# The gate z and the folded weights moved between set-up and steps of a selective state block, on one core

## What is computed

```python
def _mamba2(x, Win, Wconv, bconv, dt_bias, A_log, D, gn_w, Wout):
    zxbcdt = x @ Win
    z = zxbcdt[..., :DIN]
    xBC = silu(_causal_conv(zxbcdt[..., DIN:DIN + CONVDIM], Wconv, bconv))
    xh, Bm, Cm = ...                      # parts of xBC
    dt = softplus(zxbcdt[..., -NHEADS:] + dt_bias)
    A = -exp(A_log)
    y = _ssd(xh, dt, A, Bm, Cm) + rev(_ssd(rev(xh), rev(dt), A, rev(Bm), rev(Cm)))
    y = y + D[None, None, :, None] * xh
    y = _rmsnorm(y.reshape(b, l, DIN) * silu(z), gn_w)
    return y @ Wout
def _ssd(xh, dt, A, Bm, Cm):
    cum = cumsum(dt * A, axis=1)
    decay = where(tril, exp(cum[:, :, None] - cum[:, None, :]), 0)
    return einsum('blsh,bshp->blhp', (Cm . Bm)[..., None] * decay * dt, xh)
```

## Time and profile before

| | |
|---|---|
| median of 3 runs | 2950.7 us (2944.52 to 2956.05) |
| profiled execution, its own time | 2953.49 us |
| its span | 2951.5 us |
| PE busy | 2153.9 us (73%), weight loads 1100.1 (37%) |
| DVE busy | 1981.8 us (67%) |
| ACT busy | 1744.2 us (59%) |
| POOL busy | 1079.7 us (37%) |
| mean granted TensorE clock | 0.857 |

### The profile page before, as it was taken

The page is one execution under the profiler, slowest core; times in us unless marked ns, Lnnn a source line. Parts: engine busy times, 40 slices in busy tenths (PEclk is TensorE's granted clock), DMA queues, the critical chain, the costliest instruction groups (busy, mean ns, idle before and its releaser), DMA issues. The chain is left out here.

```text
span 2951.5 us, 64266 instructions
## 1 busy us (share of the span) xinstructions
PE 2153.9 (73%) x26182; PEld 1100.1 (37%) x26182; DVE 1981.8 (67%) x2779; ACT 1744.2 (59%) x2811; POOL 1079.7 (37%) x827
## 2 busy tenths in 40 slices
PE   4277777776774887698688588658857886885886
PEld 3022222222221553354255245325524542552553
DVE  2587888888877566565666656565765666666564
ACT  1266766766653575477367457536754773674574
POOL 0044444444451343244045235304522531451342
PEclk6588888888896998799799799869978988997998
DMA  4000000000001111110111111011111101111111
GB/s 133 0 0 1 0 1 0 1 0 0 1 0 29 32 34 28 35 33 15 44 38 26 38 27 40 15 31 32 34 36 26 42 15 39 33 25 30 32 34 31
DMA packets 96695, 74.59 MB, mean 25 GB/s; under 512 B 69392, under 2 KB 77584, under 8 KB 95120
## 3 DMA queue, kind: packets, MB, share of 16 engines
q1 hardware_dynamic: 96400, 70.48, 10.0%
HBM read 20.62 MB, written 8.39 MB: 10 GB/s over the span
## 5 line engine op out<-in xcount | busy, mean ns | idle before, releaser
L892 POOL TENSOR_TENSOR SQ<-SQ 128x512 f32<-128x512 f32 x344 | 467.2, 1360 | 708.4 <-ACT SQ L811 425.1
L859 POOL TENSOR_TENSOR Y<-Z 128x512 f32<-128x512 f32 x256 | 330.8, 1292 | 531.6 <-DVE Z L1096 297.7
L807 ACT ACTIVATE O<-bank 128x512 f32<-128x512 f32 x512 | 304.3, 594 | 210.2 <-PE bank L571 207.5
L1293 DVE TENSOR_TENSOR SQ<-bank,O 128x512 f32<-128x512 f32 x344 | 236.2, 689 | 163.8 <-issue 118.8
L571 PE MATMUL bank<-SS,work 32*128 32x512 bf16 x512 | 203.7, 398 | 169.3 <-ACT O L807 168.2
L892 POOL TENSOR_TENSOR SQ<-O,SQ 128x512 f32<-128x512 f32 x168 | 226.9, 1350 | 254.8 <-PE bank L592 185.7
L1096 DVE TENSOR_TENSOR_SCAN Z<-bank,SS 128x512 f32<-128x512 f32 x256 | 311.0, 1215 | 0.5
L536 PE MATMUL bank<-folded_weights,work 128*64 128x128 f32 x4096 | 300.1, 292 | 0.0
L463 PE MATMUL bank<-Y,constants 128*128 128x512 f32 x512 | 295.5, 662 | 6.2 <-DVE bank L1104 4.6
L592 PE MATMUL bank<-folded_weights,work 128*32 128x64 f32 x8192 | 287.3, 230 | 11.3 <-POOL SQ L892 10.8
L512 PE MATMUL bank<-XP,block_weights 128*128 128x512 f32 x256 | 156.9, 725 | 174.3 <-DVE Z L1227 174.3
(11 more groups left out here) (271 smaller groups left out, 3990.2 us busy)
## 6 DMA issues: line engine op xcount, KB each, us to landing
work<-XP SPq DMA_DIRECT2D x256, 134.0 KB
work<-extra SPq DMA_DIRECT2D x768, 8.0 KB
decay_cols_kept<-extra SPq DMA_DIRECT2D x48, 128.0 KB, 1.8
SS<-decay_cols_kept SPq DMA_DIRECT2D x384, 16.0 KB
block_weights<-callw SPq DMA_DIRECT2D x8, 735.0 KB, 4.4
Z<-state_sel SPq DMA_DIRECT2D x1, 2048.0 KB, 13.2
out<-O SPq DMA_DIRECT2D x2, 1024.0 KB, 8.5
constants<-consts SPq DMA_DIRECT2D x1, 1347.5 KB, 6.1
```

The source lines that it names most:

```text
L807: A(D2C[u % 2], bank[2], ACT.Copy).then_inc(sg("d2_copied"), 1)
L859: g.tensor_tensor(hc[t_ % 4], hs[t_ % 4], c_copy[t_ % 4], ALU.mult).then_inc(sg("s1_hc"), 1)
L892: g.tensor_tensor(MM[u % 2].rearrange("p (h l) -> p h l", l=L), DK[u % 3].rearrange("p (h l) -> p h l", l=L), GM[(u // 8) % 2][:, 64 * (u ...
L1293: v.tensor_tensor(DK[u % 3], bank[u % 2], D2C[u % 2], ALU.min).then_inc(sg("decay_least"), 1)
```

## The change

1. z: all 16 matmuls now stand in the set-up, through banks 4, 5, 7, 0 and 1 in turn. ACT copies each bank to Z2 (`copy_z`). tanh (ACT, Z2 to `tz`) and `gate_z` (DVE, Z2 in place) come once every 4 slots, -2 to 58.
2. `project_bc(0)` and `project_x(0)`, their tanh and their gates move from the slots to the set-up.
3. The folding is done in eight pieces in slots 32 to 39 of the call before, into the other of two buffers.
4. E goes: Q is made from dL and a shifted F; only F is stored (3 DMAs), and the columns of E are read out of the stored F by 3 DMAs that shift by one. The rows of Q of group 0 are issued by ACT instead of SP.
5. PE: `decay_logs(tau + 3)` becomes the last work of a slot instead of the second.

The core of the diff:

```diff
-        tz = [dte, dtr, dty]
-        def z_place(i):
-            return (i % 3, (4, 5, 7)[i % 3]) if i < 8 else (2, 7)
-        Z_SLOTS = {-8: (3, 4), -7: (5, 6), -6: (7,), -5: (8,), -3: (9,), -1: (10,), 1: (11,), 3: (12,), 5: (13,),
-                   7: (14,), 9: (15,)}
+        tz = O[:, 3584:4096]
+        z_banks = [4, 5, 7, 0, 1]
...
+        def decay_rows(eng, g, k, name):
+            for j in range(3):
+                l0 = 32 * k + 6 + 8 * j
+                for b in range(NB):
+                    rows = slice(16 * g + 8 * b, 16 * g + 8 * b + 8)
+                    eng.dma_start(LHS[g % 2][l0:l0 + 8, :].rearrange("p (u b l) -> p u b l", b=2, l=L)[:, :, b, :],
+                                  SPLIT[name][j][rows, :].rearrange("h (u l) -> h u l", l=L)).then_inc(
+                        sg(f"decay_rows{g % 2}"), 16)
+        def z_at(i):
+            return slice(TOK * (i % 2) + BANK * (i // 2), TOK * (i % 2) + BANK * (i // 2) + BANK)
+        def z_due(tau):
+            i, r = divmod(tau + 2, 4)
+            return i if r == 0 and 0 <= i < 16 else None
...
                     if g == 0:
-                        sp.wait_ge(sg("decay_stored"), (c + 1) * 96)
-                    for k in range(2):
-                        for j in range(3):
-                            r0 = 32 * k + 2 * j
-                            sp.dma_start(RHS[g % 2][r0:r0 + 2, :], cols_dram[k, j, 16 * g:16 * g + 16, :].rearrange(
-                                "(b h) n -> b (h n)", h=8)).then_inc(sg(f"decay_cols{g % 2}"), 16)
+                        sp.wait_ge(sg("split_P"), c + 1)
+                    decay_rows(sp, g, 0, "P")
+                    if g > 0:
+                        sp.wait_ge(sg("split_Q"), c + 1)
+                        decay_rows(sp, g, 1, "Q")
+                    if g == 0:
+                        sp.wait_ge(sg("decay_stored"), (c + 1) * 48)
+                    for j in range(3):
+                        kept = cols_dram[j, 16 * g:16 * g + 16, :]
+                        sp.dma_start(RHS[g % 2][2 * j:2 * j + 2, :], kept.rearrange("(b h) n -> b (h n)", h=8)).then_inc(
+                            sg(f"decay_cols{g % 2}"), 16)
+                        sp.dma_start(RHS[g % 2][32 + 2 * j:34 + 2 * j, :].rearrange("b (n l) -> b n l", l=L)[:, :, 1:L],
+                                     kept.rearrange("(b h) (u l) -> b (h u) l", h=8, l=L)[:, :, 0:L - 1]).then_inc(
+                            sg(f"decay_cols{g % 2}"), 16)
...
# PE
-                for i in range(3):
+                for i in range(5):
                     z(i)
...
+                project_bc(0)
+                project_x(0, 0)
+                project_x(0, 1)
+                for i in range(5, 16):
+                    z(i)
+                pe.wait_ge(sg("z_copied"), c * 16 + 16)
+                pe.wait_ge(sg("dt_added"), c + 1)
                 for tau in range(FIRST, LAST):
                     if 0 <= tau - 1 < L:
                         y(tau - 1)
-                    if 0 <= tau + 3 < L:
-                        decay_logs(tau + 3)
-                    for i in Z_SLOTS.get(tau, ()):
-                        z(i)
                     for half in range(2):
                         k = every(tau, 4, half - 6, 16)
-                        if k is not None:
+                        if k is not None and k > 0:
                             project_x(k, half)
                     for offset, work_ in ((-8, project_bc), (-4, scores), (12, sum_squares), (14, project_out)):
                         g = every(tau, 8, offset, NGROUP)
-                        if g is not None:
+                        if g is not None and (g > 0 or offset != -8):
                             work_(g)
+                    if 0 <= tau + 3 < L:
+                        decay_logs(tau + 3)
...
# ACT, set-up and slots
+                def copy_z(i):
+                    act.wait_ge(sg("z_psum"), c * 16 + i + 1)
+                    A(Z2[:, z_at(i)], bank[z_banks[i % 5]], ACT.Copy).then_inc(sg("z_copied"), 1)
+                for i in range(5):
+                    copy_z(i)
                 act.wait_ge(sg("dt_bounded"), c + 1)
                 A(dL, dL, ACT.Ln).then_inc(sg("dL_ready"), 1)
...
+                tanh_bc(0)
+                tanh_x(0)
+                for i in range(5, 16):
+                    copy_z(i)
+                act.wait_ge(sg("split_Q"), c + 1)
+                decay_rows(act, 0, 1, "Q")
...
+                    i = z_due(tau)
+                    if i is not None:
+                        act.wait_ge(sg("z_copied"), c * 16 + i + 1)
+                        if i >= 1:
+                            act.wait_ge(sg("z_ready"), c * 16 + i)
+                        A(tz, Z2[:, z_at(i)], ACT.Tanh, scale=0.5).then_inc(sg("z_tanh"), 1)
...
# DVE, set-up and slots
+                v.tensor_copy(grid(dQ)[:, :, 0:1], grid(dL)[:, :, 0:1])
+                order(v.tensor_tensor(grid(dQ)[:, :, 1:L], grid(dL)[:, :, 1:L], grid(dF)[:, :, 0:L - 1], ALU.add))
...
+                def gate_z(i):
+                    dve.wait_ge(sg("z_tanh"), c * 16 + (i + 1))
+                    v.scalar_tensor_tensor(Z2[:, z_at(i)], tz, 1.0, Z2[:, z_at(i)], ALU.add, ALU.mult).then_inc(
+                        sg("z_ready"), 1)
...
+                gate_b(0)
+                gate_c(0)
+                gate_x(0)
+                dve.wait_ge(sg("split_F"), c + 1)
                 for tau in range(FIRST, LAST):
+                    if 32 <= tau < 40 and c + 1 < 8:
+                        fold(c + 1, tau - 32)
...
-                    for i in Z_SLOTS.get(tau, ()):
+                    i = z_due(tau)
+                    if i is not None:
                         gate_z(i)
```

More of the change, by code:

```diff
@@ L503, in call @@
                 pe.wait_ge(sg(f"block_weights_loaded{d}"), (m * 2 + n) * 16 + 16)
+                (wxa, wxb), wbc, wog, Dhalf, bias_x, _, _, _ = folded(c)
                 def z(i):
-                    t, to = z_place(i)
-                    if i >= 8:
-                        pe.wait_ge(sg("z_ready"), c * 16 + i)
-                    elif i >= 3:
-                        pe.wait_ge(sg("z_ready"), c * 16 + (i - 2))
-                    mm(bank[to], W(f"wz{i % 2}"), xn_group(i // 2), start=True, stop=True).then_inc(sg("z_psum"), 1)
+                    if i >= 5:
+                        pe.wait_ge(sg("z_copied"), c * 16 + (i - 4))
+                    mm(bank[z_banks[i % 5]], W(f"wz{i % 2}"), xn_group(i // 2), start=True, stop=True).then_inc(
+                        sg("z_psum"), 1)
                 for g in range(4):
@@ L1141, in call @@
+            for piece in range(8):
+                fold(0, piece)
             def call(m, n, d, c):
@@ L1230, in call @@
-                for i in range(3):
-                    gate_z(i)
-                for name in ("split_P", "split_Q", "split_E", "split_F"):
-                    dve.wait_ge(sg(name), c + 1)
+                v.tensor_copy(grid(dQ)[:, :, 0:1], grid(dL)[:, :, 0:1])
+                order(v.tensor_tensor(grid(dQ)[:, :, 1:L], grid(dL)[:, :, 1:L], grid(dF)[:, :, 0:L - 1], ALU.add))
+                for name, src, ready in (("P", dP, "split_P"), ("Q", dQ, "split_Q")):
+                    hi, mid, lo = SPLIT[name]
+                    order(v.tensor_copy(hi, src))
+                    order(v.tensor_tensor(rest_v, src, hi, ALU.subtract))
+                    order(v.tensor_copy(mid, rest_v))
+                    v.tensor_tensor(lo, rest_v, mid, ALU.subtract).then_inc(sg(ready), 1)
+                    dve.wait_ge(sg(ready), c + 1)
@@ L1297, in call @@
                         k = every(tau, 4, offset, 16)
-                        if k is not None:
+                        if k is not None and (k > 0 or offset != -3):
                             work_(k)
@@ L1301, in call @@
                         g = every(tau, 8, offset, NGROUP)
-                        if g is not None:
+                        if g is not None and (g > 0 or offset > -5):
                             work_(g)
```

189 lines of the change are left out of this document (75 added, 114 removed).

## The result

The changed kernel takes 2978.4 us (median of 5 runs, 2968.3 to 2993.2) against 2950.2 for the kernel before in its 5 runs beside it. I had forecast 2841 us, faster, with a range of 2775 to 2930. Both direction and range were wrong.

The account below looks back on a forecast made before the run. No engine is near 100% busy; waits between engines, stage by stage, bound the kernel. Terms of -16.7 - 6.0 + 3.9 + 2.6 + 1 + 1.5 give -13.7 us a call, -110 over 8 calls: 2841 us, range 2775 to 2930.

Parts of the forecast that it names:

- Part A: Start of a call up to y(0): shorter DVE work and fewer DMA issues bring y(0) earlier, -16.7 us (-12 to -18).
- the z chain: Old wait before y(0): one bank goes from PE to ACT to DVE and back before PE may go on.
- the landing: Time from the last DMA issue until decay_logs(0) can go, at the start of a call: 1.8 us.
- Rival 2: DMAs at a call's start: ACT's and SP's issues take turns (+4.4), shifted columns dear (+2); 2892 us, chance 0.13.
- Part B: Loaded group of slots: PE waits for gate_x twice and gate_c once; 22.5 us against 20.9, six groups +3.9 us.
- The rule on the z gate: DVE gate with two SBUF inputs and POOL's product exclude each other: up to 1.3 us more, group 22.6 to 23.
- Clock: PE's clock dips behind waits; the new waits are shorter but more, so one dip a call, +1.5 us.
- Rival 3: Scores and output run at 1.2 GHz in each loaded group, 1.7 + 1.7 us in 48 groups; 3004 us, chance 0.10.
- First group: Group from y(0) to y(8), without squares sum and output projection yet: 19.5 us for 25.5, -6.0 us.
- Folding: Next call's folding in slots 32 to 39, some 18 short DVE instructions ahead of minima: +3 us in 7 of 8 calls.
- Tail: End of a call: one more tanh and gate, +1 us; from project_bc(7), with the sixth loaded group, +2.6 us.

Follow-up runs that it names:

- e10: The changed kernel with the three shifted column transfers of a step group written as plain ones (result not the reference's); 2954.3 us.
- e9: e7 plus one matmul with unused result, into a free bank, just before the scores of groups 1 to 7; 2942.9 us.
- e7: The changed kernel with gate_x alone moved from slots 1 and 5 to slots 0 and 4; 3073.0 us.
- e12: The changed kernel with one extra matmul, its result unused, before the scores of groups 1 to 7; 2958.4 us.
- e3: The changed kernel with gate_x moved to slots 0 and 4, and the z tanh and gate from slots 2 and 6 to 0 and 4; 2832.9 us.
- e6: e3 with the folding of the next call moved from slots 32 to 39 to slot 68; 2752.9 us.
- e8: The changed kernel with the z tanh and gate alone moved to slots 0 and 4, gate_x left in slots 1 and 5; 2880.8 us.

## Why the prediction was wrong, point by point

- **Part A, y(0): -16.7 forecast, -12.4 measured.** (1199 and 8 make 1207.0, not 1207.3, so my own terms gave -17.0.) Right: the z chain gone, z ended before the DMAs landed, ACT and SP side by side, 0.74 an issue. The last column was issued 40.6 us into the call, for my 39.2. Logs to `y(0)` took 7.9, for my 8. The term that was mis-sized here is the landing, 1.8 us taken and 5.0 measured. Its row was of stores of 128 KB to HBM; the DMAs that count are small loads into SBUF, the last of them in runs of 126 bytes. e10 shows 1.9 us of it as the price of the shift. Rival 2 had the right place, but not this mechanism: its turns of the queues did not happen, and its dear shifted DMA was dear in landing, not in issue (0.59 for my 0.74). The plain ones between them took 0.49 to 0.79, for my 0.32.
- **Part B, the loaded group: right at full clock.** 22.5 forecast, 22.55 in the changed kernel. The waits were 1.19, 1.10 and 1.05 for 1.15, 1.15 and 1.35. That the sum fits so closely is in part luck: its waits are 3.53 us in all for my 3.99, and the rest 19.0 for my 18.5.
- **The rule on the z gate.** The gate with both inputs in SBUF took 0.68 us at the least and 1.34 to 1.36 in the group shown, beside a product on POOL. The Trainium skill, "SBUF — State Buffer", section "Who interferes with whom", says that a VectorE instruction with two SBUF inputs contends with a GpSimd one that reads SBUF. The trace agrees: the long gates shown lie beside a product on POOL that began 0.47 us before them. But the full 1.3 us more that I worked out as the worst did not occur: the longest of the 128 gates took 1.36 us, 0.68 more than the shortest.
- **Clock: the step that failed.** I allowed one dip a call, +1.5 us, on the ground that "the new waits are shorter". Instead, PE's rows grew by 11.7 us a call; in c = 1 9.6 of them lie in the five loaded groups (97.0 to 106.6 us), and over all calls a loaded group without folding takes 24.2 us for my 22.5. The clock fell behind waits of 1.05 to 1.6 us, which I had called too short by comparison with 1.7 to 1.9 in the earlier trace rows. So length was the wrong ground to tell a wait that costs clock from one that doesn't. e9 shows that waits hold the clock down, since filling one gives 130 us back there, and e7 that one wait of 1.6 a group can be enough for half of a group at 1.2 GHz. Rival 3, at 0.10, was this mechanism. It put the low clock into scores and output of each group at 3.4 us a group; measured over the 33 loaded groups without folding it is 1.7 us on average, half of that: 0.4 to 0.9 in 13 groups, 1.7 to 2.2 in 11, 3.4 to 3.6 in 8 and nothing in one. The section of the Trainium skill that I had named there, "A second HAM failure mode: psum-queue depth-cycling" of "TensorE: Matmul & The Clock Gate", tells that short idle spells between groups of matmuls make the clock swing; the trace agrees, with waits of 1.05 to 1.6 us, though the same waits left some groups at 1.00.
- **First group: -6.0 forecast, -3.9 measured.** Its clock is 0.84. In calls 5 and 6 of the same execution the group has a clock of 0.98 and takes 19.9 us, so my 19.5 was nearly right at full clock, and I put the loss down to the clock again.
- **Folding: +3 forecast.** In the changed kernel removing it gave about 4 a call, close to the forecast. I take it that DVE's delay lay partly under slow PE work there, which was not tested. In e3, with the clock up, it costs 8.1 in its group and 1.2 in the next, and moving it gives 80 us, 11 a call. Folding ahead of the first call I had not counted: the norm's first reduction starts 9.9 us after the last row before it instead of 0.8, so it adds about 9 us once.
- **Tail: +2.6 forecast, +5.6 measured.** Its mean clock is 0.81, before 0.86. How much of the 3.0 us over the forecast is clock and how much the added gate was not taken apart.

Of the 14.1 us that c = 1 misses: 3.8 at the start (the landing 3.2), 6.6 in the loaded groups (their clock, with some 2 of it beside the folding), 2.1 in the first group (clock), 3.0 in the tail, less the 1.5 allowed for the clock. The clock's share is inferred from the stretch tables for the changed kernel; shown by experiment is that filling waits raises the clock (e9, and by little e12) and that taking the waits away does (e3, e6). What decides which group of the changed kernel dips and which does not is open.

## What to carry to other kernels

A wait placed into a matmul stream has two prices: its length, which distances between rows gave here to 0.1 us for all but one (1.05 for my 1.35), and the clock behind it. Here the clock came to 1.7 us for 3.5 us of waits in the changed kernel's mean group, and to three times the wait in most calls of e7. So when a change trades one long stall for several short ones, price the work behind each short one at the lower clock as well, and compare a group only with a group at the same granted clock. And judge edits in pairs: `gate_x` alone made the kernel 3% slower than the changed one, the z gates alone 3% faster, both together 5% faster, because only both together brought all the waits of an ordinary group below 0.6 us.

## What the runs showed of the hardware

- PE waits of 1.05 to 1.6 us were followed by stretches of 3 to 14 us at 1.2 GHz, though not each of them: the kernel before has waits of 0.67 and 1.72 us in groups at 1.00, and e8 has waits of 1.19 and 1.10 us in every group and most of its groups are at 1.00. In e7 the dip came in group after group, at the same place, in five of the eight calls. In e6, whose waits are 0.53, 0.19 and 0.44 us, the loaded groups shown had none.
- An extra matmul of 1.13 us in a wait of 1.6 us raised the mean clock of a group from 0.75 to 1.00 and shortened it by 4.8 us.
- Small column loads landed 3.1 us after the last issue in plain form and 5.0 us when half of them were copied in runs of 126 bytes, where a store of 128 KB showed 1.8. Issue was 0.25 to 0.54 us for a plain one in e10, 0.49 to 0.79 for a plain one between shifted ones, 0.58 to 0.60 for a shifted one.
- Two engines that issued six row DMAs each took 4.49 and 4.36 us at the same time, no longer than one alone (0.74 each).
